# Two depthwise convolutions on one core: conv 2's row blocks gathered by way of a zero-padded DRAM scratch

## The reference, cut to what matters

```
x: (8, 384, 128, 128) f32,  k1: (384, 1, 3, 3),  k2: (384, 1, 7, 7)

_gn(v, G=32): per image and group of 12 channels: (v - mean) / sqrt(var + 1e-5)

x = x + depthwise_conv3x3(_gn(x), k1, pad 1)
w_sym = (k2 + rot90(k2, 1) + rot90(k2, 2) + rot90(k2, 3)) * 0.25
x = x + depthwise_conv7x7(_gn(x), w_sym, pad 3)
```

## Time and profile before

| | us |
|---|---|
| median of 3 runs | 3548.77 (3547.64 to 3551.12) |
| the profiled execution's own time | 3551.22 |
| its span in the profile | 3549.4 |
| TensorE (PE) busy, matmuls | 2933.2 (83% of the span) |
| VectorE (DVE) busy | 2254.7 (64%) |
| ScalarE (ACT) busy | 2173.1 (61%) |
| GpSimd (POOL) busy | 1565.6 (44%) |

### The profile page before, as it was taken

The page is one execution under the profiler, slowest core; times in us unless marked ns, Lnnn a source line. Parts: engine busy times, 40 slices in busy tenths (PEclk is TensorE's granted clock), DMA queues, the critical chain, the costliest instruction groups (busy, mean ns, idle before and its releaser), DMA issues.

```text
span 3549.4 us, 86790 instructions
## 1 busy us (share of the span) xinstructions
PE 2933.2 (83%) x28676; PEld 1667.2 (47%) x28676; DVE 2254.7 (64%) x4988; ACT 2173.1 (61%) x3969; POOL 1565.6 (44%) x1552
## 2 busy tenths in 40 slices
PE   0568888879888889888888888888988888988896
PEld 0235544445454445544445444444544544544453
DVE  3546656666666666666667666666666666666663
ACT  1446656566566666666567666666666656666672
POOL 3324444444444444444445445444444435444452
PEclk9789999999999999999989899999998999999998
DMA  7798888878888888888888888888888988888887
GB/s 132 184 243 250 247 244 243 251 224 251 247 247 247 243 249 243 250 248 250 245 246 250 244 239 252 249 246 245 252 244 235 258 235 257 246 248 249 251 238 202
DMA packets 1081258, 853.90 MB, mean 241 GB/s; under 512 B 204344, under 2 KB 990776, under 8 KB 1080664
## 3 DMA queue, kind: packets, MB, share of 16 engines
q1 hardware_dynamic: 675224, 646.03, 65.5%
q10 hardware_dynamic: 405504, 201.38, 20.0%
HBM read 262.32 MB, written 221.88 MB: 136 GB/s over the span
## 4 chain that ended last, share of the span: by engine, by line
PE 53%; SPq 22%; issue 14%; DMA 5%; POOL 3%; DVE 3%; ACT 0%; ACTq 0%; POOLq 0%; DVEq 0%
PE PS L718 27%; PE PS L690 24%; SPq L230 16%; DMA BT<-H 4%; SPq L239 4%; POOL H L611 3%; SPq L258 2%; PE PS L655 0%; DVE X L364 0%; PE PS L662 0%; DMA rows<-v_all 0%; ACTq L542 0%; ACT TMP L546 0%; DVE TMP L418 0%; DVE H L457 0%
## 5 line engine op out<-in xcount | busy, mean ns | idle before, releaser
L718 PE MATMUL PS<-BT,BAND 126*32 126x512 f16 x21504 | 1343.6, 411 | 439.7 <-issue 333.2
L690 PE MATMUL PS<-H,BAND 128*128 128x512 f16 x6912 | 1574.0, 387 | 115.2 <-issue 56.5
L619 POOL TENSOR_TENSOR H<-Z,H 128x512 f16<-128x512 f32 x768 | 865.7, 1130 | 1289.1 <-ACT Z L531 1270.2
L718 PEld LDWEIGHTS PS<-BT,BAND 126*32 126x32 f16 x21504 | 785.9, 133 | 992.1 <-issue 553.8
L690 PEld LDWEIGHTS PS<-H,BAND 128*128 128x128 f16 x6912 | 860.2, 127 | 777.9 <-issue 133.6
L611 POOL TENSOR_SCALAR H<-X,RB 128x512 f16<-128x512 f32 x768 | 674.7, 893 | 652.2 <-DVE RB L424 416.8
L528 ACT ACTIVATE H<-X,RB 128x512 f16<-128x512 f32 x768 | 618.3, 805 | 219.6 <-DVE H L457 214.7
L511 ACT ACTIVATE Z<-X,RB 128x512 f32<-128x512 f32 x768 | 561.4, 802 | 104.1 <-DVE RB L424 91.9
L531 ACT ACTIVATE Z<-X,RB 128x512 f32<-128x512 f32 x768 | 615.1, 801 | 0.0
L554 ACT ACTIVATE DUMP<-X 128x512 bf16<-128x512 f32 x768 | 476.3, 621 | 158.6 <-DVE X L484 158.4
L435 DVE SCALAR_TENSOR_TENSOR X<-PS,SC,X 128x2048 f32<-128x2048 f32 x192 | 451.4, 2351 | 188.7 <-PE PS L718 177.0
(11 more groups left out here) (45 smaller groups left out, 359.6 us busy)
## 6 DMA issues: line engine op xcount, KB each, us to landing
BT<-H SPq DMA_DIRECT2D x1152, 174.6 KB
X<-in_x SPq DMA_DIRECT2D x768, 256.0 KB, 4.0
out_y<-X ACTq DMA_DIRECT2D x768, 256.0 KB, 4.8
BT<-H SPq DMA_DIRECT2D x1152, 149.6 KB
BAND<-rows SPq DMA_DIRECT2D x96, 220.5 KB
rows<-v_all SPq DMA_DIRECT2D x8, 1764.0 KB, 11.8
BAND<-rows SPq DMA_DIRECT2D x192, 51.0 KB, 2.9
BAND<-rows SPq DMA_DIRECT2D x192, 49.5 KB, 3.1
```

What stands on the lines that cost most here:

```text
L619: g.tensor_tensor(part(H1, n, 1, img, O1, P1), Z[:, img, :].rearrange("p (c w) -> p c w", c=CC), part(H1, n, 0, img, O1, P1), ALU.subtract ...
L690: last = mm(PA[:, ch, :], band[:, j, ws, :], data[:, :, O1 - 1 + j:O1 - 1 + j + W], start=k == 0, stop=k == 3 * K1 - 1)
L718: last = mm(banks2(n)[b * BL:(b + 1) * BL, ch, :], band[:, j, :], rows, start=j == 0, stop=j == K2 - 1, tile_position=(0, b * BL))
```

## The change

Between `H2` and `BT` stands a scratch in DRAM, `staged`, with two buffers, a high and a low part each, and 138 rows: 128 of data and five rows of zeros above and below. SP writes each part to it as one DMA of 128 rows (`stage`), waits for its landing, and then fills `BT` with three DMAs, one for each term, in each of which the four overlapping blocks of 42 rows are read from DRAM. The zero rows are written once at the start. The memset of `BT` goes, and the zero rows of the first and last block are now copied with the others. GpSimd now waits for the two writes of chunk n-2 and no longer for its gather. The wait for conv 2 of chunk n-2 stands between the writes and the reads.

```diff
-EDGE = 36
-LANDED = 16 * TERMS * NB
+LANDED = 16 * TERMS
+ROWS = P + 2 * HALO
...
+    staged = nc.dram_tensor("staged", (2, 2, ROWS, CC * L2), F16, kind="Internal").ap()
...
-            def window(b):
-
-                top = b * BL - HALO
-                lo_row, hi_row = (0, EDGE) if b == 0 else (P - EDGE, P) if b == NB - 1 else (top, top + WIN)
-                return lo_row, hi_row, lo_row - top
+            def stage(n, which, done):
+
+                q = n % 2
+                sp.dma_start(staged[q, which, HALO:HALO + P, :],
+                             H2[:, q, which, :, :].rearrange("p c l -> p (c l)")).then_inc(done[q], 16)
 
             def gather(n, k):
 
                 q, which = n % 2, (0, 1, 0)[k]
-                for b in (0, 2, 1, 3):
-                    lo_row, hi_row, r0 = window(b)
-                    first = TERMS * r0 + k
-                    sp.dma_start(BT[first:first + TERMS * (hi_row - lo_row - 1) + 1:TERMS, q, b, :, :],
-                                 H2[lo_row:hi_row, q, which, :, :]).then_inc(gathered[q], 16)
+                rows = staged[q, which, 0:WIN, :]
+                rows = bass.AP(rows.tensor, rows.offset, [[CC * L2, WIN], [BL * CC * L2, NB], [1, CC * L2]])
+                sp.dma_start(BT[k:KW:TERMS, q, :, :, :].rearrange("p b c l -> p b (c l)"),
+                             rows).then_inc(gathered[q], 16)
...
                 n = t - 3
                 if real(n):
-                    if n < 2:
-                        sp.wait_ge(blocks_zeroed, 1)
+                    q, turn = n % 2, (at(n) - n % 2) // 2
+                    if n >= 2:
+                        wait_apart(sp, gathered[q], turn * LANDED)
                     else:
+                        sp.wait_ge(halo_zeroed, 64)
+                    wait_apart(sp, hi_done[1], NI * at(n) + NI)
+                    stage(n, 0, high_staged)
+                    wait_apart(sp, lo_done[1], NI * at(n) + NI)
+                    stage(n, 1, low_staged)
+                    if n >= 2:
                         wait_apart(sp, conv2_done, at(n) - 1)
-                    wait_apart(sp, hi_done[1], NI * at(n) + NI)
+                    wait_apart(sp, high_staged[q], turn * 16 + 16)
                     gather(n, 0)
                     gather(n, 2)
-                    wait_apart(sp, lo_done[1], NI * at(n) + NI)
+                    wait_apart(sp, low_staged[q], turn * 16 + 16)
                     gather(n, 1)
...
                 if n >= 2:
-                    wait_apart(pool, gathered[n % 2], ((at(n) - n % 2) // 2) * LANDED)
+                    wait_apart(pool, high_staged[n % 2], ((at(n) - n % 2) // 2) * 16)
+                    wait_apart(pool, low_staged[n % 2], ((at(n) - n % 2) // 2) * 16)
+                if n == 0:
+                    pool.wait_ge(halo_zeroed, 64)
...
-                if t == 1:
-
-                    pool.wait_ge(vectors_stored[1], 16)
-                    g.memset(flat32(BT[:]), 0.0).then_inc(blocks_zeroed, 1)
```

More of the change, by code:

```diff
@@ L127, in conv_program @@
         vectors_stored = [sem("vectors_stored1"), sem("vectors_stored2")]
-        blocks_zeroed = sem("blocks_zeroed")
         passed = sem("passed")
@@ L132, in conv_program @@
         stored = [sem(f"stored{r}") for r in range(BODY)]
+        high_staged = [sem(f"high_staged{q}") for q in range(2)]
+        low_staged = [sem(f"low_staged{q}") for q in range(2)]
+        halo_zeroed = sem("halo_zeroed")
         gathered = [sem(f"gathered{q}") for q in range(2)]
@@ L313, in _ @@
             cut1(1, G)
+            sp.wait_ge(zeroed, 10)
+            for rows in (slice(0, HALO), slice(HALO + P, ROWS)):
+                for q in range(2):
+                    sp.dma_start(staged[q, :, rows, :].rearrange("s r l -> r s l"),
+                                 H2[0:HALO].rearrange("p a s c l -> p (a s c l)")[:, 0:2 * CC * L2]
+                                 .rearrange("p (s l) -> p s l", s=2)).then_inc(halo_zeroed, 16)
             walk(sp, slot)
```

## The result

| | before | changed |
|---|---|---|
| device time, median | 3548.2 us | 3906.3 us |
| lowest to highest of 4 runs | 3543.14 to 3551.12 | 3897.61 to 3913.63 |
| ratio, 95% interval | | 1.101 [1.0986, 1.1035] |
| profiled execution | 3551.2 us | 3913.44 us |
| its span | 3549.4 us | 3911.6 us |

The changed kernel is 10.1% slower. I had said 3500 us, at most 3720, so both the sign and the range missed.

The account below looks back on a forecast made before the run. It took SP's nearly full issue queue to bound the kernel before, and DMA afterwards: 17.0 us transfers plus 0.3 idling gave 17.3 us a chunk against 17.54, 46 us less, so 3500 us; range 3420 to 3541, whole 3330 to 3720.

Parts of the forecast that it names:

- Reading of the kernel before: TensorE's work alternates with waits for what SP issues; SP's queue nearly full, twelve copies taking 9.1 to 14 us a chunk.
- long gap: Wait at a unit's first chunk: 8 us backlog in SP's queue, 14 us issuing, 3.4 us to the landing.
- share of 0.87: DMA engines' mean share at 246 GB/s in the kernel before; much of the packets' time in it said to be waiting.
- SP's issues: Two writes at 0.40 and three reads at 0.86, 3.4 us a chunk, replace twelve copies and remove the 8 us backlog.
- GpSimd and the bytes: GpSimd's 235.0 us of gather waits go, costed at nothing; bytes rise from 853.9 to 1092.5 MB, 5.69 MB a chunk.
- I take 335: DMA engines become the bound, moving 5.69 MB a chunk at 335 GB/s, so 17.0 us a chunk.
- The idling of the round trip: Engines idle between the write's last packet and the first read's: 0.3 us a chunk, 2.4 us if standing open.
- Latency of a gather: From low part done to last landing: 15 to 16 us through DRAM, against 17 before without the backlog.
- A: Slower rival: engines can't be kept at 335 GB/s, a chunk takes 18.1 to 18.2 us, 3665 us in all; chance 0.33.
- B: Much slower rival: reads stay at 225 GB/s, slowed by writes into BT's interleaved partitions; 4040 us; chance 0.06.
- signs that I named for A or B: Reads over 20 us from issue to landing, or stretches with only reads in flight under 300 GB/s.
- C: Much faster rival: packets quicker, DMAs at 358 GB/s need 15.9 us, latency's 16.2 us holds; 3294 us; chance 0.16.

Follow-up runs that it names:

- Experiment 9: The kernel before with each of its copies moving two of the four channels, so half the gather's bytes: 3316.76 us, ratio 0.9338.
- experiment 4: The kernel before with two writes of all rows to DRAM added behind its twelve copies, read by nobody: 4140.14 us, ratio 1.1653.
- experiment 1: The changed kernel with SP issuing the writes first and the next input loads between writes and reads: 3856.95 us, 1.0868 of the kernel before.
- experiment 2: The changed kernel with four scratch buffers, reads taking rows written two chunks before, so none waits for a fresh write: 3794.43 us, 1.0687 of before.
- experiment 5: The changed kernel with only the first chunks written, terms interleaved in the scratch, one read filling 128 neighbouring partitions: 3055.63 us, 0.8608 of before.
- experiment 6: The changed kernel with only the first chunks written, terms interleaved in the scratch, one read filling the 126 needed partitions: 3283.27 us, 0.9242 of before.
- experiment 7: The complete changed kernel with interleaved scratch, three writes, loads between writes and read, one read over 128 partitions: 3545.12 us, 0.9993 of before.
- experiment 10: As experiment 7, but SP's order as in the change, loads ahead of the writes: 3967.17 us, 1.1162 of the kernel before.
- experiment 3: The changed kernel with only the first two chunks written to the scratch, the reads going on as before: 3347.87 us, 0.9436 of the kernel before.

## Why the prediction was wrong

**Reading of the kernel before: half right.** I had it bound by SP's issuing, with a backlog in SP's queue. Experiment 9 confirms that in part (half of the long gap stays at half the bytes) and adds what I left out: 234 us hung on the bytes of the gather. From the share of 0.87 I had said that much of the packets' time was waiting and that the engines were far from full. That is not settled: taking bytes away paid at once in experiment 9, and experiment 4, which adds some, can't tell, since its loss lies in SP's queue. I also read the long gap, 10.11 us in the earlier trace rows, as that of every unit's first chunk; it is that of every second unit.

**SP's issues: right in the median, short in the sum.** I had 3.4 us a chunk. Issue durations in the changed kernel (min/median/max, ns) give 2 x 0.502 + 3 x 0.794 = 3.4:

```profile
L234 SPq DMA_DIRECT2D BT<-staged x576: 788/794/2177, 167.3 to 3885.4; - x192
L226 SPq DMA_DIRECT2D staged<-H x384: 320/502/5710, 160.0 to 3873.5; - x192
L243 SPq DMA_DIRECT2D X<-in_x x768: 372/776/11231, 1.6 to 3742.5; - x192
```

But long issues are frequent: from 200 us on, the two writes and three reads take SP 4.8 us a chunk in the mean, and the four loads, unchanged in number and size, 4.5 instead of 1.9 (the third line, against the earlier trace rows). I had put that rise at nothing. Of the time that is freed, 5.5 us a chunk are then spent standing in front of landings. The zero rows' writes at the start, also put at nothing, may be the 5.9 us by which the first conv 2 starts later (179.7 against 173.8); no run parts that.

**GpSimd and the bytes: right.** The 235 us of waits became 6.4, and the change moves 1093.24 MB where I had 1092.5.

**The step that failed: "I take 335".** The prediction's term was 5.69 MB / 0.335 = 17.0 us a chunk. In the steady stretch the change moves 286 GB/s, and with SP's wait for the landing or the dependence taken away 290 to 295, at a share of 1.00 to 1.01. At 286 GB/s and (3903.2 - 179.7) / 192 = 19.39 us a chunk, that is 5.55 MB a chunk (my 5.69 had spread the transfers of the start over the chunks as well). 5.55 MB need 19.1 us at experiment 1's 290, and 16.6 at my 335. So the rate was short by 2.5 us a chunk, the bytes were too many by what is worth 0.4, and the term was 2.1 too small: some 400 us of the 406 by which I missed. By experiment 2's 295 it is 18.8 us, 1.8 too small, and the round trip has the rest.

Experiments 5 to 7 show where the rate went: I took the rate of 8 us in which three quarters of the bytes were loads and stores over 128 partitions (2.0 of 2.7 MB), and gave it to a mix with reads over 42. My reason for 335, that the new transfers are more like those loads and stores, is what experiments 5 and 6 speak against: the two partitions alone are worth at least 228 / 192 = 1.2 us a chunk. Of the estimated 1.8 us between 36 packets of 206 ns and 32 of 176 (experiments 6 and 5), 0.8 are the four packets more on an engine, and 1.0 that each packet runs longer. This is shown apart only in kernels without writes. In the complete kernel experiment 7 changes the partitions, the number of reads and the scratch's layout together, and a version with 126 partitions wasn't run there.

**The idling of the round trip, 0.3 us a chunk:** 49 / 192 = 0.26 by experiment 1, 112 / 192 = 0.6 by experiment 2. That it looks almost right is luck: I had the low write and the stores fill the time to the landing, and they don't (32 and 45 GB/s in the windows above). It costs little because another bound hid it; where the reads go over 128 partitions it is up to 422 / 192 = 2.2 us (experiment 10), close to the 2.4 that I had as the price of an open round trip. I also let a write land in 5.6 us, and it takes 7.8 in the median.

**Latency of a gather:** I had said 15 to 16 us without the backlog, so that the gap at a unit's first chunk would shrink to 1 to 4 us. It is 10.19 us in the timeline, and in the median of every second unit 8.8 us as before. A landing of 7.8 us, and 11 to 12 us in the median from the first read's issue to the last one's landing, take what the queue gave.

**The rivals.** A named the half-open round trip and reads that run slower than at 335 GB/s, and its sign was right; it joined them by "or", at 3665. They came together, and larger, so that the result lies between A and B's 4040, nearer to B. B's own mechanism, that slow writes into interleaved partitions hold the reads back, is there at most as the 65 us, or 0.34 a chunk, between experiments 3 and 6. I gave A 0.33, and the 0.54 for faster rested on one window of 8 us. Of the signs that I named for A or B, the reads' time of over 20 us didn't come (15.6 at most); the last sentence of the prediction, that it is wrong if the largest wait is one for `staged`, is what the chain shows. And the whole range began at 3330 us, above C's own 3294.

**Open.** Why the same 4256 bytes take 162 ns at the least but 176 to 228 in the mean is measured and not explained. From 126 to 128 partitions both the number of packets that are most often on their way at once, 14 to 16, and their mean length, 206 to 176 ns, change, and no run parts the two. What holds experiment 7 at 352 GB/s isn't known either. A version with fewer bytes, which might beat the kernel before, wasn't tried: experiment 5 leaves the writes out, and so says only that three reads' worth of DRAM traffic fits under TensorE's work.

## What to carry to other kernels

Take a sustained rate only from a stretch whose transfers have the same shape as the new ones (the steady stretches here hold 273 to 295 GB/s with reads over 42 partitions, and 299 to 352 with reads over 128), and count in the trace how many of their packets are on their way at once. Where a DMA goes over 126 partitions, moving two useless rows more can be the faster choice (228 us of 3283 here). When data goes out to DRAM and comes back through one queue, put transfers that nobody waits for between the write and the read, not ahead of the write (worth 422 us between experiments 10 and 7, and 49 between the change and experiment 1); and when undoing one suspected wait brings little, undo the second as well before you acquit the first.

## What the runs showed of the hardware that I had not expected

- A DMA share of 1.00 is no rate. It stood at 1.00 with 290 GB/s (experiment 1), 0.98 with 273 (experiment 3) and 1.05 with 352 (experiment 7), each over 2000 us.
- The time to landing of one and the same write of 532 KB is 5.3 us in the median as an addition to the kernel before (experiment 4), 7.8 in the change and 9.4 with loads issued behind it (experiment 1). In these runs the landing isn't a property of the transfer, but goes with what is in flight around it, behind it included.
- Adding 209 MB of writes over 128 partitions cost 446 us, which is 469 GB/s at the margin, more than any stretch shown here moves in sum. No run shows why. (Some of them may have gone into time in which experiment 3 waited for TensorE, so the price is a lower bound.)
- The issue of an unchanged load got slower with the traffic: 0.401 us in the median before, 0.776 in the change.
- Moving four of twelve copies from SP to GpSimd made the kernel 4.2% slower. Their packets took 259 ns against 235 for SP's in the same kernel, but the run doesn't part that from GpSimd's wait for TensorE.
